# Combined quarters of x: plain sums by accumulating transfers in place of differences on VectorE

## What is computed

```
h = gelu(x @ fc1_w.T + fc1_b)                      # 512 -> 2048
shared = h @ fc2_w.T + fc2_b                       # 2048 -> 384
expert = h @ experts_w[idx[b]].T + experts_b[...]  # 2048 -> 128
x = x + concat(shared, expert)
scores = tanh(x @ W1 + b1) @ v                     # one per token
mask = l <= j, l >= j or l != j, by pt[b]
x = x + (softmax(where(mask, scores, -1e30)) @ x) / count(mask)
```

## Time and profile before

| | us |
|---|---|
| median of 3 runs (1314.91 to 1315.12) | 1315.1 |
| profiled execution | 1315.22 |
| its span, first to last instruction | 1313.4 |
| PE busy | 1307.3 |
| DVE busy | 1086.4 |
| ACT busy | 953.8 |
| POOL busy | 165.0 |

### The profile page before, as it was taken

How to read it: one execution, slowest core, us unless ns; L and a number is a source line. 1 busy time by engine, 2 the same in 40 slices (tenths; PEclk the granted TensorE clock), 3 DMA queues, 4 the chain that set the end, 5 groups by cost and what they waited for, 6 DMA issues and landing times.

```text
span 1313.4 us, 24064 instructions
## 1 busy us (share of the span) xinstructions
PE 1307.3 (100%) x9261; PEld 906.8 (69%) x9261; DVE 1086.4 (83%) x2080; ACT 953.8 (73%) x1716; POOL 165.0 (13%) x272
## 2 busy tenths in 40 slices
PE   9999999999999999999999999999999999999998
PEld 5448476585867858577685866858678585876856
DVE  7998998778969688796977969789696987869798
ACT  5868858588585876958679596886858779586762
POOL 0000000030200203011030200303002030110302
PEclk9999999999999999999999999999999999999999
DMA  8411021040220402113030220312113021130206
GB/s 301 144 57 34 1 65 33 7 112 23 50 70 33 97 33 45 53 47 84 32 74 25 55 76 33 89 33 49 57 39 92 33 57 41 49 96 3 67 19 121
DMA packets 38165, 79.71 MB, mean 61 GB/s; under 512 B 7058, under 2 KB 8482, under 8 KB 35618
## 3 DMA queue, kind: packets, MB, share of 16 engines
q1 hardware_dynamic: 28834, 61.65, 14.4%
q0 software_dynamic: 8640, 15.73, 7.3%
q10 hardware_dynamic: 576, 0.79, 0.2%
HBM read 45.65 MB, written 18.87 MB: 49 GB/s over the span
## 4 chain that ended last, share of the span: by engine, by line
PE 99%; DVE 0%; ACT 0%; issue 0%; DVEq 0%
PE ps L483 14%; PE ps L485 14%; PE ps L484 14%; PE ps L568 10%; PE ps L570 10%; PE ps L569 10%; PE ps L579 6%; PE ps L587 6%; PE ps L590 6%; PE ps L650 1%; PE ps L648 1%; PE ps L647 1%; PE ps L465 1%; PE ps L469 1%; PE ps L467 1%; PE ps L454 1%
## 5 line engine op out<-in xcount | busy, mean ns | idle before, releaser
L483 PE MATMUL ps<-xh,w1h 128*128 128x256 f16 x960 | 261.7, 273 | 0.0
L484 PE MATMUL ps<-xl,w1h 128*128 128x256 f16 x960 | 261.7, 273 | 0.0
L485 PE MATMUL ps<-xh,w1l 128*128 128x256 f16 x960 | 261.7, 273 | 0.0
L934 ACT ACTIVATE g<-ps,b1s,ds 128x512 f32<-128x512 f32 x240 | 173.6, 774 | 71.6 <-PE ps L485 71.6
L483 PE MATMUL ps<-xh,ch 128*128 128x256 f16 x720 | 196.4, 273 | 0.0
L485 PE MATMUL ps<-xh,cl 128*128 128x256 f16 x720 | 196.2, 273 | 0.0
L484 PE MATMUL ps<-xl,ch 128*128 128x256 f16 x720 | 196.2, 273 | 0.0
L1496 DVE SCALAR_TENSOR_TENSOR hl<-g,ix,hh 128x512 f16<-128x512 f32 x243 | 176.0, 745 | 3.0
L909 ACT ACTIVATE hh<-g,ix 128x512 f16<-128x512 f32 x243 | 161.5, 718 | 0.0
L570 PE MATMUL ps<-hl,w2h 128*128 128x512 f16 x384 | 145.5, 379 | 0.0
L568 PE MATMUL ps<-hh,w2l 128*128 128x512 f16 x384 | 145.5, 379 | 0.0
(11 more groups left out here) (345 smaller groups left out, 2779.9 us busy)
## 6 DMA issues: line engine op xcount, KB each, us to landing
space<-in_xT SPq DMA_DIRECT2D x62, 256.0 KB, 3.1
er<-in_ew SPq DMA_DIRECT2D x15, 1024.0 KB, 4.8
out<-space SPq DMA_DIRECT2D x60, 256.0 KB, 2.8
space<-space POOLq DMA_DIRECT2D x52, 256.0 KB, 3.4
space<-in_w SPq DMA_DIRECT2D x29, 256.0 KB, 6.0
er<-in_w SPq DMA_DIRECT2D x3, 1024.0 KB, 9.4
out<-sums POOLq DMA_DIRECT2D x8, 255.5 KB, 5.4
space<-in_ew SPq DMA_DIRECT2D x1, 1024.0 KB, 6.3
```

The costliest lines, as they stand in the source:

```text
L483: mm(to, wh, mh, start=i in (1, 5) and c == 0, stop=False, skip_group_check=True)
L484: mm(to, wh, ml, start=False, stop=False, skip_group_check=True)
L485: m = mm(to, wl, mh, start=False, stop=c == 1, skip_group_check=True)
L934: act(in_two(g_of(b, k)), src, ACT.Gelu, bias=b1s[:, k:k + 1], scale=ds1[:, b % 2, p:p + 1]).then_inc(gelu_done)
```

## The change

The four combined quarters of batch b + 1 are made by DMA. SP copies one quarter into each place (`put_quarters`), in the order T3, T1, T2, T4, each when `hl` of tile 12, 13, 14 or 15 of batch b is written. POOL issues an accumulating transfer for each (`sum_quarters`): T3 = X22 + X12, T1 = X12 + X11, T2 = X11 + T3, T4 = X21 + T2 (the first term is what was put). They are plain sums now, so the signs in two additions of products (`add_first`, `add_second`) and in two sums of weights change. The order of the splits becomes X11, X21, T3, T1, T2, X22, T4. `combine` goes from DVE's program. `put_quarters(1)` stands in SP's program between the reloads of w1 and the load of w2's chunk 2; `put_quarters(b + 1)` at the end of SP's batch b (for b = 1 ahead of the first store). `sum_quarters(1)` to `(3)` stand ahead of all of POOL's program, `sum_quarters(n + 3)` behind `mend(n)`. Four small tables share one semaphore, `tables_in`, waited for at 64.

```diff
-    X_ORDER = (X11, T1, T2, X21, T3, X22, T4)
+    X_ORDER = (X11, X21, T3, T1, T2, X22, T4)
+    PLACES = (T3, T1, T2, T4)
+    PUT_FIRST = {T3: (1, 1), T1: (0, 1), T2: (0, 0), T4: (1, 0)}
@@
-        return in_two(g[:, t - T1, :])
+        return in_two(g[:, PLACES.index(t), :])
@@ gelu_pair
-                    e.wait_ge(xl_done, nth_x(b, T1 + k))
-                    e.wait_ge(combos, 4 * b)
+                    e.wait_ge(xl_done, nth_x(b, PLACES[k]))
+                    for t in (T1, T4):
+                        e.wait_ge(*combined_by(b, t))
@@ split_x_high
-                e.wait_ge(combos, 4 * (b - 1) + t - T1 + 1)
+                e.wait_ge(*combined_by(b, t))
@@ split_x2_high
-                e.wait_ge(xl_done, nth_x(b + 1, (T2, T4)[n - 1]))
+                e.wait_ge(xl_done, nth_x(b + 1, (T1, T4)[n - 1]))
+                e.wait_ge(*combined_by(b + 1, (T2, T4)[n - 1]))
@@ vector_program
-            tt(combined(t), x, y, ALU.subtract).then_inc(combos)
@@ add_first (add_second alike)
-            tt(half_bank(y, 1), half_bank(y, 0), fifth[:, p % 2, :], ALU.add).then_inc(added0)
+            tt(half_bank(y, 1), fifth[:, p % 2, :], half_bank(y, 0), ALU.subtract).then_inc(added0)
@@ static_columns
-            e.wait_ge(vcol_in, 16)
+            e.wait_ge(tables_in, LOADED)
@@ sync_program
+        def put_quarters(b):
+            for c in range(KD):
+                e.wait_ge(x_in[b % XB * KD + c], x_loaded(b))
+            for n, t in enumerate(PLACES):
+                e.wait_ge(hl_done, nth_tile(b - 1, NH - GR + n))
+                dma(combined(t), quarter(b, *PUT_FIRST[t])).then_inc(put_by(t), 16)
@@
         for k in range(PLAIN, NH):
             e.wait_ge(hl_done, nth_tile(0, k))
             dma(w1r[k], w1[:, k, :]).then_inc(w1_in[k], 16)
+        put_quarters(1)
         e.wait_ge(w2l_done, nth_chunk(0, 3))
         dma(er[:, 0, :], w2[:, 2, :]).then_inc(e_in[0], 16)
@@
             if b == 1:
+                put_quarters(2)
                 store(0, 0)
@@
+            if 1 < b < LAST:
+                put_quarters(b + 1)
@@ gpsimd_program
+        def sum_quarters(b):
+
+            for t, x in ((T3, quarter(b, 0, 1)), (T1, quarter(b, 0, 0)), (T2, combined(T3)), (T4, combined(T2))):
+                e.wait_ge(put_by(t), nth_put(b, t))
+                if t in (T2, T4):
+                    e.wait_ge(*combined_by(b, T3 if t == T2 else T2))
+                eng.dma_start(combined(t), x, accum_op=ALU.add).then_inc(combined_by(b, t)[0], 16)
+
+        for n in (1, 2, 3):
+            sum_quarters(n)
         for n in range(1, LAST - 1):
             mend(n)
+            if n + 3 <= LAST:
+                sum_quarters(n + 3)
```

More of the change, by code:

```diff
@@ L297, in build @@
                                        sems("ein", 2), sems("ebin", 2))
[L298 to L301, removed]
+    (e0_in, idx_in, pt_in, b1_in, b2_in, aw_in, av_in, tables_in, eye_in) = (
+        sem(n) for n in ("e0in", "idxin", "ptin", "b1in", "b2in", "awin", "avin", "tablesin", "eyein"))
+    LOADED = 16 * 4
+    vmax_done, atth_done, attl_done, x2_step, x2_scaled = (
+        sem(n) for n in ("vmax", "atth", "attl", "x2step", "x2scaled"))
     (bits_set, summed, tile_done, p1, p5, p6, p7, p3, fc2_done, half_done, attended, score_done, nat_done, cols_done,
@@ L324, in build @@
     first_added, second_added = sems("firstadd", 2), sem("secondadd")
+    t3_put, t1_put, others_put, t1_done = (sem(n) for n in ("t3put", "t1put", "othersput", "t1"))
     mend_step, turned_done, s_done, s_copied, s_step = (sem(n) for n in ("mend", "turned", "corr", "corrcopy", "corrstep"))
@@ L372, in nth_x, with put_by, nth_put, combined_by @@
         return 7 * (b - 1) + X_ORDER.index(t) + 1
+    def put_by(t):
+        return {T3: t3_put, T1: t1_put}.get(t, others_put)
+    def nth_put(b, t):
+        return 16 * b if t in (T3, T1) else 32 * b
+    def combined_by(b, t):
+        return (t1_done, 16 * b) if t == T1 else (combos, 16 * (3 * (b - 1) + (T3, T2, T4).index(t) + 1))
     def nth_w1(k):
@@ L1058, in tanh @@
             e.wait_ge(attended, nth_chunk(b, KD - 1))
-            e.wait_ge(ab_in, 16)
+            e.wait_ge(tables_in, LOADED)
             if b:
@@ L1234, in scalar_program @@
         split_expert_high(0, 3)
-        for t in (T1, T2, X21, T3, X22, T4):
+        for t in X_ORDER[1:]:
             split_x_high(1, t)
@@ L1272, in scalar_program @@
                 one_way_exponentials(b - 1)
-                for t in (X11, T1, T2):
+                for t in (X11, X21, T3):
                     split_x_high(b + 1, t)
                 split_x2_high(b, 0)
-                split_x_high(b + 1, X21)
+                split_x_high(b + 1, T1)
                 evacuate(b, 3)
@@ L1279, in scalar_program @@
                 inverses(b - 1)
-                split_x_high(b + 1, T3)
+                split_x_high(b + 1, T2)
                 split_x2_high(b, 3)
@@ L1293, in scalar_program @@
             split_x_high(b + 1, X11)
+            split_x_high(b + 1, X21)
+            split_x_high(b + 1, T3)
             split_x_high(b + 1, T1)
-            split_x_high(b + 1, T2)
-            split_x_high(b + 1, X21)
             if scanned_once(b - 1):
@@ L1300, in scalar_program @@
             seed(b, 3)
-            split_x_high(b + 1, T3)
+            split_x_high(b + 1, T2)
+            split_x2_high(b, 1)
             split_x_high(b + 1, X22)
-            split_x2_high(b, 1)
             split_x_high(b + 1, T4)
@@ L1317, in see @@
             e.wait_ge(shift_done, 1)
-            e.wait_ge(io_in, 16)
+            e.wait_ge(tables_in, LOADED)
             e.wait_ge(p3, nth_pair(LAST, PAIRS - 1))
@@ L1549, in add_second @@
             e.wait_ge(p7, nth_pair(b, p))
-            tt(half_bank(x, 1), half_bank(y, 0), fifth[:, p % 2, :], ALU.add).then_inc(added1)
+            tt(half_bank(x, 1), fifth[:, p % 2, :], half_bank(y, 0), ALU.subtract).then_inc(added1)
         def x2_low(b, c):
@@ L1646, in weight_sums_first @@
             e.wait_ge(w1l_done, NH)
-            tt(v[3], v[2], v[3], ALU.add).then_inc(sums_step)
+            tt(v[3], v[2], v[3], ALU.subtract).then_inc(sums_step)
             e.wait_ge(sums_step, q + 1)
@@ L1655, in weight_sums_second @@
             e.wait_ge(sums_step, q + 3)
-            tt(v[1], v[1], v[0], ALU.subtract).then_inc(sums_step)
+            tt(v[1], v[1], v[0], ALU.add).then_inc(sums_step)
         def sums_low(p):
@@ L1714, in places @@
             first, p = io[0:ROWS3, 0:4], lcol[0:ROWS3, 0:1]
-            e.wait_ge(lcol_in, 16)
-            e.wait_ge(io_in, 16)
+            e.wait_ge(tables_in, LOADED)
+            e.wait_ge(tables_in, LOADED)
             e.wait_ge(mask_step, 13)
@@ L2102, in vector_program @@
         batch_scales(1)
-        combine(1, T1)
-        combine(1, T2)
         expert_low(0, 1)
@@ L2108, in vector_program @@
         ts(vscaled[:, :], vcol[:, :], scale_of(vc), None, ALU.mult).then_inc(vmax_done)
-        combine(1, T3)
-        combine(1, T4)
         expert_low(0, 2)
-        x_low(1, T1)
-        x_low(1, T2)
+        x_low(1, X21)
+        x_low(1, T3)
         expert_low(0, 3)
         sums_low(1)
-        for t in (X21, T3, X22, T4):
+        for t in X_ORDER[3:]:
             x_low(1, t)
@@ L2175, in vector_program @@
             if paired(b):
-                for t in (T1, T2, T3, T4):
-                    combine(b + 1, t)
                 bounds(b + 1)
@@ L2183, in vector_program @@
                 x_low(b + 1, X11)
+                x_low(b + 1, X21)
+                x_low(b + 1, T3)
                 x_low(b + 1, T1)
+                third_sum(b, hl)
                 x_low(b + 1, T2)
-                x_low(b + 1, X21)
-                third_sum(b, hl)
-                x_low(b + 1, T3)
                 x2_low(b, 3)
@@ L2229, in vector_program @@
             x_low(b + 1, X11)
+            x_low(b + 1, X21)
+            x_low(b + 1, T3)
+            pool(rest[1])
             x_low(b + 1, T1)
+            pool(rest[2])
             x_low(b + 1, T2)
-            pool(rest[1])
-            x_low(b + 1, X21)
-            pool(rest[2])
             x2_low(b, 1)
-            x_low(b + 1, T3)
             x_low(b + 1, X22)
@@ L2397, in sync_program @@
         dma(pts[:, :], pt).then_inc(pt_in, 16)
[L2398 to L2401, removed]
+        dma(abs_[:, :], ab).then_inc(tables_in, 16)
+        dma(vcol[:, :], av[:, 0:1], allow_slow_non_contiguous=True).then_inc(tables_in, 16)
+        dma(io[:, :], iota).then_inc(tables_in, 16)
+        dma(lcol[:, :], tokens).then_inc(tables_in, 16)
         dma(fifth[0:E, 0, 0:P], eb).then_inc(b2_in, 16)
```

## The result

The changed kernel takes 1319.27 us (median of 9 runs, 1317.35 to 1320.44) against 1315.1 of before: a ratio of 1.0031, interval 1.0022 to 1.0040. It is 4.2 us slower. Its profiled execution took 1318.77 us, with a span of 1317.0, 3.6 us more than before.

What follows compares the result with a forecast made beforehand. PE at its own rate was taken to bound the kernel. At the start, 3.2 us of puts plus 3.2 of sums less 2.2 free gave 4.2, so 1319.3 us against 1315.1; range 1316.2 to 1323.1.

Steps and rivals of the forecast that it cites:

- The place of the loss: Batch 0, chunk 1: PE's chain_sum(8) waits for DVE's L1414, this for er<-in_w; each us of later landing costs one.
- the puts' time on the engines: At the start, four puts ahead of er<-in_w on its queue take 3.2 us of the 16 engines.
- the term of the engines: At the start, puts 3.2 us plus two POOL sums of 1.6 each, less 2.2 free: er<-in_w 4.2 us later.
- The issues on SP: Four puts issued before er<-in_w make its issue 1.1 to 2.3 us later, at 58.4 to 59.6, not 57.30.
- The steady batches: Puts and sums in later batches stay hidden, slack 7.6, 9.7 and over 6 us for T3, T2, T4: cost 0.
- The step that failed: In steady batches, T1's sum was timed from its own put, to be there by 705.5 at the latest.
- A: Rival at the start: er<-in_w waits only for its issue, landing 1.1 to 2.6 us later, say 1316.8 us; chance 0.23.
- point of decision: What separates A from the forecast: er<-in_w landing 2.6 us later, that is, before or after 67.9.
- The prediction's own sign of being wrong: At the start: the forecast is wrong if er<-in_w lands at or before 67.9; about 4 us of PE idle expected.
- B: Rival at the start: er<-in_w's landing, or what PE waits for, does not move; no cost, 1315.1 us; chance 0.03.
- C: Rival: DVE's 41 us come back, at most PE's waits of 1.1, 0.3 and 0.14 us, 1313.6 us; chance 0.03.
- D: Rival: sums over 7.6 us stall PE in 12 steady batches; at 9 us each, 17 us more, 1336 us; chance 0.05.

Runs made afterwards that it cites:

- e10: e5 with every put of a batch held until hl of tile 15 is written: 1318.56 us, ratio 1.0026.
- e5: The changed kernel with the puts of batch 1 issued only when er<-in_w has landed, behind the expert's load: 1314.94 us, ratio 0.9999.
- e2: The kernel before with only the four puts added ahead of er<-in_w, no sums by POOL, DVE still combining: 1316.29 us, ratio 1.0009.
- e3: The changed kernel with POOL's first sum held until er<-in_w has landed, puts unmoved: 1316.12 us, ratio 1.0008.
- e1: The changed kernel with the puts of batch 1 moved behind the issue of er<-in_w on SP: 1316.05 us, ratio 1.0007.
- e8: The kernel before with er<-in_w's issue held until the second quarter of w2's chunk 1 is split, no puts or sums: 1316.43 us, ratio 1.0011.
- e9: The kernel before with er<-in_w's issue held until all of w2's chunk 1 is split, no puts or sums: 1319.24 us, ratio 1.0029.
- e4: The changed kernel with 20 unused matmuls of 256 columns filling PE's wait ahead of chain_sum(8): 1317.48 us, ratio 1.0018.
- e6: e5 with the last two reloads of w1 (tiles 14 and 15) also behind er<-in_w's landing: 1314.97 us, ratio 0.9999.
- e7: e4 with 10 filler matmuls in place of 20: 1317.35 us, ratio 1.0018.

## Why the prediction was right, and where it was not

*What bounds the kernel.* Right. PE's period stayed 79.60 us in every version but e10, and DVE's 37 us (41 foretold) bought nothing: e5 has all of the change but its place on SP's queue, at 1314.94.

*The place of the loss.* Right: er<-in_w, L1414, chain_sum(8). The forecast that each us of er's landing is a us of PE held wherever the clock stayed up: L1414 later by 0.79, 0.91, 0.90, 1.19 us in e2, e3, e1, e8, and the times 1.2, 1.1, 1.0, 1.3 us up. In the changed kernel and in e9, where the clock fell, it cost one and a half times to twice as much (L1414 2.0 and 2.7 us later, 4.2 and 4.1 us up). Nothing was given back later.

*Its size.* The total, 4.2 us, was met; its terms were not. The sum put 3.2 us for the puts' time on the engines, 3.2 for two sums, less 2.2 of free time, and none for the clock. Measured: er's landing moves by 2.0 us, of which the puts make 0.9 (e3) and T3's sum 1.1 (the changed kernel against e3); the lower clock makes 1.7 to 1.8 (e4). Two errors met, and that together they give the 4.2 us of the forecast is luck. First, the term of the engines was twice too large. I took er's 8.0 us as its own, and only 4.8 are: e8, e9 and e6 show 4.8 or 4.9 when nothing stands ahead, and the other 3.1 were time behind w1's reloads, into which later issues fall for nothing. That is why e2's 2.9 us of later issue cost 0.8. I also put T1's sum into er's time, but POOL issues it only when T3's has landed (e10 above); T3's took 8.3 us beside er, and T1's came at 69.17, when er had landed. Second, a step was missing: what PE's clock does after an idle stretch. The page of before shows a full clock throughout, and I did not ask what a first stretch of idle would do to it.

*The issues on SP.* Mis-sized: 0.34 us each at least, I said, 2.63 us for four at the most; they took 2.96, with a median of 0.62 us for one put. er was issued at 60.01, past my latest 59.6. That should have cost nothing by itself: with the 4.8 us of e8 from there er would land at 64.9 (an estimate), before the 65.3 of the kernel before.

*The rules weighed.* Of the Trainium skill, DMA: Bandwidth & Descriptors, section Queues, rings and completion order, the rule that a ring is served in order agrees with e1 and e2 only in part: the puts ahead of er cost 0.8 us, the puts behind it 0.9, so it matters little which side they are on. The rule of Issuing engines are not separate DMA queues, that all issuers share the 16 engines, agrees with e3: one sum by POOL beside er costs 1.1 us. With the fabric figure of that page of the Trainium skill for the puts (the estimate of 2.4 us) the sum would have been 3.4 us, above the 2.0 measured as well.

*The steady batches.* The forecast, no cost, was right; the slack was not. T3's cover is 6.7 us (sum there at 708.9, split at 715.56), near the 7.6 foretold, but T1, which I had ready by 705.5, comes at 713.1 with all times 3.6 us later, 709.5 on the times of before. The step that failed let T1's sum follow its own put; it follows the landing of T3's sum. e10 shows what that is worth.

*The rivals.* A asked for er's landing within 2.6 us, and it was: 2.0. By its point of decision it would have been the case, with 1317.1; e4, at 1317.48, is that case, though puts and sum did delay er, which A had denied. The prediction's own sign of being wrong thus came true: er landed at 67.3, before 67.9, and PE stood idle for 2.1 us, not for about 4. Only the clock, which neither the forecast nor a rival had, carried the time to that of the forecast. B, C and D did not occur.

## What to carry to other kernels

Where TensorE sets the time, a change that relieves another engine has nothing to win and is judged by what its transfers delay: look for the one load on which TensorE already stands, and keep new transfers out of its way by a wait on its landing, not by their order of issue (e1 against e5). A stall of TensorE may cost nearly twice its length, so price it with the clock that follows, and ask whether filler matmuls, or removing half of the stall, keep it. The landing of a transfer is not its own duration: take it from a place where nothing stands ahead. And where two transfers bear the same name in a wait, look at each one's landing before you say which ended it.

## What the runs showed of the hardware

- With PE idle for 0.7 to 1.2 us (e1, e2, e3, e7, e8) the granted clock stayed at 2.4 GHz; after 2.1 and 2.5 us (the changed kernel, e9) it fell to 1.2 GHz soon after PE had resumed, which cost 1.7 us in the changed kernel, in 8 of 9 and 7 of 10 runs by their times. These are the stretches that occurred here; what lies between them was not tried.
- A transfer of 1 MB from HBM landed after 4.8 us alone (e8, e9), 8.0 us when issued right behind two of 256 KB (before; 4.9 without the two, e6), 9.0 with four of 256 KB behind it as well (e1), and 7.3 with four ahead and an accumulating one beside it (6.1 without that one, e3).
- SP was kept 0.62 us (median) by the issue of a put of 256 KB from SBUF with two runs in each partition, 0.34 us by that of a load of 256 KB from HBM with one. The shape is not all: the issue of er, the same in both, took 0.34 us in the kernel before and 0.70 us right behind four puts.
- In batches 2 to 15 of the changed kernel the puts of T3 and T1, issued ahead of the sums, landed after 2.5 to 3.0 us; those of T2 and T4, in flight together with T3's sum, after 2.6 to 5.7 us.
- An accumulating transfer of 256 KB within SBUF landed after 3.3 us at least, 3.9 in the median, and 8.3 beside the load of 1 MB.
